# A vision transformer on one core: the next image's first two heads scored within FF2, the head loop two heads ahead, and an opening in another order

## What is computed

```python
h = tok(x)                                   # Haar analysis, three levels, gates, synthesis
h = concat([cls_tok, h], axis=1)             # B=8, S=257, D=256
x = layernorm(h)
for i in range(4):                           # H=16 heads of DH=64
    q, k, v = split(x @ W_qkv[i])
    kr = r @ W_r[i]                          # positions
    AC = einsum('bqhd,bkhd->bhqk', q + u, k)
    BD = einsum('bqhd,khd->bhqk', q + v, kr)
    prob = softmax((AC + BD) / sqrt(DH))
    x = layernorm(x + (prob @ v) @ W_o[i])
    ff = relu(x @ W_ff1[i] + b_ff1[i]) @ W_ff2[i] + b_ff2[i]     # DF=1024
    x = layernorm(ff)
h = h + x
h = h + experts(layernorm(h))                # 8 experts in 4 groups, routed by two gates
```

## Time and profile before

| | us |
|---|---|
| median of 3 runs | 2518.98 |
| lowest, highest | 2518.2, 2522.68 |
| the profiled execution, whole | 2520.23 |
| its span, from first to last instruction | 2518.4 |

### The profile page before, as it was taken

How to read it: one execution, slowest core, us unless ns; L and a number is a source line. 1 busy time by engine, 2 the same in 40 slices (tenths; PEclk the granted TensorE clock), 3 DMA queues, 4 the chain that set the end, 5 groups by cost and what they waited for, 6 DMA issues and landing times.

```text
span 2518.4 us, 61172 instructions
## 1 busy us (share of the span) xinstructions
PE 2224.4 (88%) x19318; PEld 1661.3 (66%) x19318; DVE 1848.3 (73%) x5687; ACT 1601.8 (64%) x4853; POOL 1190.4 (47%) x2205
## 2 busy tenths in 40 slices
PE   0249999999989999999989999999899999988998
PEld 0127777777767777777767777777677777765665
DVE  8837777777767777777757777777678888886543
ACT  2217777777767777776757777776667777665322
POOL 3015555555456555554545555554565555541211
PEclk9679999999999999999999999999999999999999
DMA  5354444445554444444644444455533343355110
GB/s 167 84 147 105 122 102 112 112 109 149 154 146 121 108 110 110 109 123 141 187 125 117 112 102 116 105 149 148 158 97 93 100 107 97 98 146 185 52 47 22
DMA packets 378059, 295.35 MB, mean 117 GB/s; under 512 B 45087, under 2 KB 350721, under 8 KB 376739
## 3 DMA queue, kind: packets, MB, share of 16 engines
q1 hardware_dynamic: 370603, 272.41, 41.4%
q10 hardware_dynamic: 4864, 12.68, 1.5%
q0 software_dynamic: 2272, 6.35, 0.7%
HBM read 137.71 MB, written 72.07 MB: 83 GB/s over the span
## 4 chain that ended last, share of the span: by engine, by line
PE 36%; ACT 23%; DVE 13%; POOL 7%; issue 6%; SPq 5%; DMA 4%; DVEq 0%; POOLq 0%; ACTq 0%
ACT e_rows L2162 11%; PE bk L2064 5%; PE bk L2076 5%; PE bk L2033 4%; PE bk L1279 4%; PE bk L1905 4%; ACT pt L2147 4%; SPq L1538 3%; DVE x L2419 3%; DVE o_rows L2327 2%; ACT rel L2097 2%; PE bk L1893 2%; PE bk L1844 2%; POOL arena L1732 2%; POOL arena L1730 2%
## 5 line engine op out<-in xcount | busy, mean ns | idle before, releaser
L2162 ACT ACTIVATE e_rows<-e_rows,nb 128x257 f32<-128x257 f32 x1024 | 516.4, 515 | 47.7 <-DVE nb L2356 47.1
L2356 DVE CUSTOM_DVE_ANT_0 e_rows<-bk,arena 128x257 f32<-128x257 f32 x1024 | 390.1, 418 | 81.2 <-PE bk L1938 79.8
L1844 PE MATMUL bk<-hin,arena 128*128 128x257 f16 x3072 | 424.9, 276 | 18.2 <-DMA hin<-hd_dram 8.8
L2318 DVE TENSOR_TENSOR pt<-bk,pt 128x512 f16<-128x512 f32 x512 | 353.7, 691 | 64.4 <-ACT pt L2147 51.6
L1893 PE MATMUL bk<-ident,e_rows 128*128 128x128 f32 x2048 | 324.1, 281 | 49.5 <-ACT e_rows L2162 28.2
L1732 POOL TENSOR_TENSOR arena<-rel,arena 128x257 f16<-128x257 f32 x496 | 328.3, 662 | 41.4
L1844 PEld LDWEIGHTS bk<-hin,arena 128*128 128x128 f16 x3072 | 298.5, 98 | 69.6 <-issue 17.1
L1730 POOL TENSOR_SCALAR arena<-rel 128x257 f16<-128x257 f32 x496 | 203.6, 410 | 273.0 <-ACT rel L2097 264.9
L2147 ACT ACTIVATE pt<-bk 128x512 f16<-128x512 f32 x512 | 310.2, 606 | 7.2 <-PE bk L1893 7.2
L1893 PEld LDWEIGHTS bk<-ident,e_rows 128*128 128x128 f32 x2048 | 221.5, 141 | 135.1 <-ACT e_rows L2162 113.0
L1937 PE MATMUL bk<-arena 128*128 128x257 f16 x1024 | 256.7, 275 | 11.7 <-DMA arena<-arena 11.2
(11 more groups left out here) (329 smaller groups left out, 4181.7 us busy)
## 6 DMA issues: line engine op xcount, KB each, us to landing
arena<-arena SPq DMA_DIRECT2D x768, 128.5 KB
wf<-in_w_dram SPq DMA_DIRECT2D x168, 128.0 KB, 2.9
w_split_dram<-wh SPq DMA_DIRECT2D x168, 128.0 KB, 2.3
xs_dram<-in_c_blank_dram SPq DMA_DIRECT2D x24, 772.5 KB
wf<-in_we_dram SPq DMA_DIRECT2D x96, 128.0 KB, 2.7
we_split_dram<-wh SPq DMA_DIRECT2D x96, 128.0 KB, 2.0
w_rest<-w_split_dram SPq DMA_DIRECT2D x12, 1024.0 KB, 17.2
arena<-we_split_dram SPq DMA_DIRECT2D x8, 1536.0 KB, 12.3
```

Of the source, the lines that this page charges most:

```text
L1844: r_ = mm(bank[4 + s % 2][:, 0:S], wcol(a, C_QKV, k, 3 * HD, chunk_at(s)), hin[:, m, k, :], start=i == 0, stop=i == 5)
L2162: act.activation(E[:, h % EB, qt, :], E[:, h % EB, qt, :], ACT.Exp, bias=nb[:, 2 * h + qt:2 * h + qt + 1], scale=-1.0, accum_out=sums[:, q ...
L2318: v.tensor_tensor(pt[:, h, 1, :, 0:IMG], bank[2 + h % 2][:, :].rearrange("p (k s) -> p k s", k=QT), pt[:, h, 0, :, 0:IMG], ALU.subtract).t ...
L2356: v.tensor_tensor_reduce(E[:, h % EB, qt, :], bank[qt][:, 0:S], cb[:, h, :], -SCORE, 3e38, ALU.add, ALU.min, nb[:, 2 * h + qt:2 * h + qt + ...
```

## The change

In the attention stage:

- `AHEAD = 2`. In slot h of the head loop PE scores head h + 2, DVE takes the maxima of h + 2, ACT the exponentials of h + 2; all three do it in loops that now transpose and copy head h itself (`transposes(at, h)`, `p_part(at, h)` on ACT) or head h - 1 (DVE).
- Heads 0 and 1 of the next image are scored within FF2 of this one: 4 products ahead of the last 6 of FF2's first output half, 4 ahead of the last 6 of its second. DVE takes their maxima in a row behind `class_q`; ACT takes the exponentials of head 0 ahead of the two squares and those of head 1 behind them. For image 0 they are in the prologue.
- `stack_in` becomes two semaphores, so that scores of heads 0 to 7 wait for the first 12 transfers alone.
- The end of the loop: `last_sums` stands in slot 14 of DVE; the last head's transposes stand in slot 14 of PE, in front of the last projection; the transposes of sums and class column stand in front of the product of heads 2 and 3 (in TAIL and FINAL of heads 0 and 1 too).
- In ENTRY the second LayerNorm's normalising and gain stand together in slot 4 of POOL, its halves in 6 and 7 instead of 9 and 10, and `class_v` two slots earlier.
- On DVE `sum_squares` stands behind both of FF2's outputs instead of between them.

In the opening:

- POOL makes no more low halves of weights; DVE makes all seven, six ahead of its LayerNorm and one behind. ACT takes the means out of two blocks, with 8 + 1 + 8 instructions of 256 columns for each. The blocks come in the order 5, 6, 3, 0, 1, 2, 4, and the last four are loaded once DVE has freed a buffer.
- `hs` lies in the same memory as `pt`, which both stages now share. `token_stage` doesn't wait for its store to DRAM any more (`hd_first` is waited for later), and image 0's `hin` is copied from there.
- PE does `class_v` ahead of the wait for the constants; ACT waits for the position term's way through DRAM after three queries instead of ahead of the first.

```diff
@@ token_stage
-        BY_POOL = C_1 // 2048
+        CHUNKS = (5, 6, 3, 0, 1, 2, 4)
-            sp.dma_start(io["hd"]..., hs...).then_inc(hd_out, 16)
-            sp.wait_ge(hd_out, 16)
+            sp.dma_start(io["hd"]..., hs...).then_inc(keep["hd_first"], 16)
...
-            for i in range(BY_POOL):
...
-                pool.tensor_tensor(w_part(W, 1, c.start, c.stop), t, w_part(W, 0, c.start, c.stop), ALU.subtract).then_inc(w_lo, 1)
...
+            def centre_weights(i):
+                act.wait_ge(w_in[i % NS], 16 * (i // NS + 1))
+                t = wst[:, i % NS, :].rearrange("p (j c) -> p j c", c=SPLIT)
+                for j in range(CJ):
+                    act.activation(t[:, j, :], t[:, j, :], ACT.Identity, accum_out=wmean[:, i, j:j + 1]).then_inc(w_sum, 1)
+                act.activation(wmean[:, i, :], wmean[:, i, :], ACT.Copy, scale=-1.0 / SPLIT).then_inc(w_sum, 1)
+                for j in range(CJ):
+                    act.activation(t[:, j, :], t[:, j, :], ACT.Identity, bias=wmean[:, i, j:j + 1]).then_inc(w_centred, 1)
...
-            for i in range(BY_POOL, NW):
+            for i in range(2 * NS):
                 split_weights(i)
             v.wait_ge(h0_in, 16 * 5)
             layer_norm_rows(v, step, xt, xt, stats, mv, rstd, var_ok, y0_ok)
             v.sem_inc(xn_ok, 1)
+            split_weights(2 * NS)
@@ attention_stage, sync
-            sp.dma_start(flat(hin), io["hd"][0]).then_inc(hin_in, 16)
+            sp.dma_start(flat(hin), p_flat[:, 0:2 * KC * S]).then_inc(hin_in, 16)
@@ tensor
+            def scores(at, h):
+                if h in (0, NP):
+                    pe.wait_ge(stack_in[h // NP], at(192, 192))
+                for qt in range(QT):
+                    if h:
+                        pe.wait_ge(s_ok, at(32, 2 * h + qt - 1))
+                    q = qs[:, h, qt * P:(qt + 1) * P]
+                    mm(bank[qt][:, 0:S], q, kh[:, h, :], start=True, stop=False)
+                    mm(bank[qt][:, 0:S], q, kl[:, h, :], start=False, stop=True).then_inc(s_done, 1)
...
-                pe.wait_ge(stack_in, at(384, 384))
                 for h in range(H):
-                    for qt in range(QT):
...
+                    if h + AHEAD < H:
+                        scores(at, h + AHEAD)
...
-                    if h:
-                        transposes(at, h - 1)
+                    if h < H - 1:
+                        transposes(at, h)
+                    if h == H - 2:
+                        if not kind.routes:
+                            values_free(at, atl, b, kind)
+                            pv(at, 0)
+                        transposes(at, H - 1)
...
                 for m_, cs in ((0, range(FC - 2)), (1, range(FC - 2)), (0, range(FC - 2, FC)), (1, range(FC - 2, FC))):
+                    if kind.next and cs.stop == FC:
+                        if m_ == 0:
+                            pe.wait_ge(v_lo, at1(4, 4))
+                        scores(at1, m_)
@@ scalar
+                    if h + AHEAD < H:
+                        exponentials(at, h + AHEAD)
...
-                    if h:
-                        p_part(at, h - 1)
+                    p_part(at, h)
...
                 if kind.next:
                     v_part(at1, 2)
                     v_part(at1, 3)
+                    exponentials(at1, 0)
...
+                if kind.next:
+                    exponentials(at1, 1)
@@ vector
+                    maxima(at1, 0)
+                    maxima(at1, 1)
                 if kind.routes and kind is not FINAL:
                     route_normalise(v, r, b - 1)
...
                 for m in range(KC):
-                    if m == KC - 1:
-                        sum_squares(sq2_ok, at(2, 2), sum2_ok)
...
+                sum_squares(sq2_ok, at(2, 2), sum2_ok)
```

241 lines of the change are left out of this document (130 added, 111 removed).

## The result

The changed kernel takes 2511.09 us, the kernel before beside it 2520.21; the ratio is 0.9965 with a 95% interval of 0.9955 to 0.9974. So it is faster by 9 us, 0.35%, where 57 were forecast, and the time lies 14 us above the range. The profiled execution has a span of 2510.5 us.

What follows compares the result with a forecast made beforehand. No single engine was the bound; a MIDDLE body's head loop was taken as ACT's, with PE carrying the rest. Gains of 25 + 21.6 + 10 + 2 - 2, about 57 us, from 2520.23 gave 2463 us, range 2438 to 2497.

Steps and rivals of the forecast that it cites:

- the opening: Everything up to the first scores: 25 us gained, as 4 + 7.7 + 5 + 8, bounds 15 and 30.
- the stackings: Prologue: two semaphores let scores of heads 0 to 7 go sooner; 10 us less 2 for heads 8 on.
- The first step: Opening's first part: DVE's stalled gate products go, 15.4 us, less 11 of weight transfers; 4 gained, bounds 0 and 12.
- the three terms: Opening: 4 from stalled gate products, 7.7 from hin copied on chip, 5 from ACT's later wait for the position term.
- the start of the boundary: MIDDLE body: FF2 ends 0.89 us later, and ec, the class row's exponential, starts about 1.8 behind it, 0.97 later than now.
- ACT's loop: MIDDLE body: class row's exponential to head 15's exponentials' end falls from 28.28 to 25.46 us.
- the step from 3.18 to 3.85 us: MIDDLE body: last exponentials to first normalising copy of the outputs grows to about 3.85 us through three copies of P.
- TAIL and FINAL: Seven bodies: boundary gives back DVE's loop gain, the end of the loop gains 1.5 us each, bounds 0 and 2.5; 10 gained.
- ENTRY: Three bodies: early LayerNorm puts about 1.2 us on POOL ahead of SP's stacking; 0.7 lost each, 2 in all.
- CLOSING: Three bodies: PE's loop has 0.89 us less, FF2 0.89 more, partly beside waiting for hin; 0.7 gained each, 2 in all.
- (a): Rival, chance 0.22: opening gains, but ec 2 us later and a tail 0.7 longer eat the loop's gain; 2495 or 2485.
- MIDDLE's: Attention stage, 18 bodies: net 1.2 us gained per body, 21.6 in all, bounds 9 and 36.

Runs made afterwards that it cites:

- b2: Kernel before with the opening changes alone, a single stacking semaphore and its one-head loop; ratio 0.9944 to the kernel before.
- a1: Changed kernel with the opening of the kernel before: the attention stage's changes alone, two semaphores included; ratio 1.0015 to the kernel before.
- f3: f2 with body 0's load of the next image's hin issued three weight chunks sooner; body 1 from 68.3 to 64.2 us, the sum down by 6.5.
- n_before: Kernel before without the second product of each score (stacked q with the low half of stacked k), so less exact; MIDDLE bodies 64.77 us.
- e5: Changed kernel with heads 0 and 1 scored at the start of their own body instead of within FF2; MIDDLE bodies 65.85 us.
- e1: Changed kernel with DVE's copy of head 14's transposes ahead of the last key; MIDDLE bodies 64.45 us, where the changed kernel has 64.93.
- e2: Changed kernel with the last head's transposes put back behind the last projection on PE; MIDDLE bodies 64.46 us, where the changed kernel has 64.93.
- f2: Changed kernel with last transposes behind the last projection, DVE's copy of head 14 ahead of the last key, and routing rows loaded early; MIDDLE bodies 64.40 us.
- f4: f3 with DVE's three key instructions ahead of its copy of head 15; 2485.54 us, 1.5% below the kernel before.
- f1: Changed kernel with PE's last projection, last transposes, then product of heads 0 and 1, and routing rows loaded early; MIDDLE bodies 64.83 us.
- e6: Changed kernel with ENTRY's second LayerNorm steps and class values in their old slots; ENTRY bodies 77.86 us instead of 76.80.

## Why the prediction was wrong

**Right: the opening.** 25 us were forecast, 25.9 were found at the end of body 0. b2's body 0 is 16.6 shorter (4 + 7.7 + 5 = 16.7 forecast for what it has), a1's 9.1 (8 forecast for the stackings). The first step fits: the tokens are stored 14.6 us sooner (at 68.51 instead of 83.06), but the issue of the loads behind ends only 3.4 sooner (97.03 instead of 100.42), so the transfers ate 11.2, where 11 were forecast. That LayerNorm also gained about what was forecast, 3.9, is in part luck: the prediction took it to wait for the tokens, and it stood behind DVE's own work, which the new order of the blocks took away. Further on two errors cancel. The first stacking starts 20.5 us sooner (141.09 instead of 161.57), where the three terms make 16.7, and then takes 13.44 us instead of 9.72, which was not foreseen; why it is slower was not tried. What was missed is behind it: body 1 gives back 4.5, since its `hin` comes through SP's queue and a fallen clock follows the wait, and f3 gets it back with one number. The prediction moved image 1's `hin` along with the stacking but did not follow image 2's, which body 1 reads, through POOL's chunks to FF2's end.

**Right: the start of the boundary and ACT's loop.** Scores in FF2 wait for nothing; ec 1.74 us behind FF2 (1.8); the exponentials of head 15 end 27.2 us behind FF2's end (27.27). n_before shows that the loop is not PE's, e5 that it is ACT's.

**Wrong: the tail of a MIDDLE body, the step from 3.18 to 3.85 us.** It is 5.23. The 1.38 us per body over 18 bodies are 25 us, half of the miss. The sum went through ACT's three copies of P and left out what PE and DVE have in their queues there. On DVE the change puts the last transposes in front of the last projection, and the last key waits for that projection with two copies and `pkr` behind it. The prediction named what is queued behind a wait in FF2, and did not do so here. e1, e2 and f2 show this as the cause for 0.5 us of the 1.38. The rest, 0.9, is still there in f2 to f4. By the traces it is PE's queue: the transposes of head 14, the last projection and a third product group now come behind the last exponentials, and in f4 PE works through them without a gap. That part is read from the rows and not tested by a run.

**Wrong in sign: TAIL and FINAL, forecast -10, found +8.8.** The forecast let the boundary give back all that the loop gains and took "the end of the loop" as a gain of 1.5 per body. The loop gained 4.7, the boundary gave back 0.6 of it, and the end of the loop is where TAIL loses: it grew by 2.9. In its rows the last transposes wait for DVE's copies, and PE has no product to fill the wait. The second cause, the rows' landing, was in the trace of before, as a wait of 3.57 us on DVE that cost nothing. The prediction didn't read that row. f1 and f2, which have the order of e2 on PE and the early rows, bring TAIL down to 66.17 and 66.54.

**ENTRY: size right, reason not shown.** +0.8 per body (0.7 forecast), and the early LayerNorm does put the stacking 1.2 us back. But with the old slots (e6) ENTRY is no shorter, so that is not what it lost by. The waits show what did grow: `vbd` comes 43.6 to 44.3 us into the body, as before (43.5 to 44.2), so the shorter loop only makes PE wait longer for it, 6.3 to 7.0 us instead of 2.8 to 4.2. Since the mean of three bodies moves by 0.7 between runs of the same code, that the size fits may be luck.

**CLOSING.** -0.7 was forecast and -0.1 found. The loop is PE's, as read. That what leaves it comes back whole in FF2, with nothing of it hidden beside the wait for the next `hin`, is the likely reason; no run tested it.

**The rivals.** (a) with its 2495 was nearest: the boundary and the tail eat the loop's gain. It gave the tail 0.7 more where 1.38 were lost, and it let TAIL come out even; its other half, ec 2 us later, did not happen (1.74 behind FF2), so it was near by half of its mechanism. The range ended 14 us too low because TAIL's bound was put at 0 to 2.5 us of gain, with no loss in it, although DVE was known to be the bound there, and MIDDLE's at 9 to 36 us of gain, where 7 were lost, 4.5 of them in body 1.

## What to carry to other kernels

When a loop is made to run further ahead, the work at its end is not just the last slot moved: list on every engine what stands between the last producer and the first consumer behind the loop, in the new order, and look for an instruction that waits for another engine with urgent ones behind it. A wait that costs nothing because something else ends at the same time is the next bound as soon as the something else moves; such waits are to be read in the trace of before and priced. When a sum of several edits disappoints, splitting it by body kind tells more than the total: here two edits of one change were worth +1.06 and -0.92 per body. And a wait of PE can cost more than its length: look at the granted clock behind it.

## What the runs showed of the hardware

The issue of the tokens' four loads stretched from 6.24 to 14.53 us once weight blocks of 1 MB were loaded beside them (2.8 MB in that stretch), while the throughput rose from 194 to 292 GB/s: the transfers shared the time and were not queued one behind the other.

A TensorE that is busy for 95% of a stretch by the records, at a granted clock of 1.00, gave back 0.02 us when 3.55 us of its 61.7 were taken away.

A PE that had stood still for 3.76 us (body 1) and for 2.99 us (a TAIL body) went on at a granted clock of about 0.5 and was back at 1.00 within 4 us; 2.2 us of standing still in the last TAIL body and 1.3 in the kernel before were followed by no fall. In ENTRY, behind the waits for `vbd` (6.3 to 7.0 us in the changed kernel), the clock is low for longer.
